# Conv-attention hybrid on one core: who takes the exponentials of the late rounds, where the gate's products stand, and the second norm in five chains

## The chip, the core and the metric

The kernel runs on one core of a Trainium2 chip: TensorE (matrix products, transposes), VectorE, ScalarE (functions from tables, copies), GpSimd and SyncE (transfers), each with its own queue in program order, joined by semaphores. The metric is the device time of one execution in microseconds. All data is float32.

## What is computed

Two images of 32 x 32 tokens with 128 channels go through three stages. The first is neighbourhood attention (7 x 7 window, 8 heads of 16 channels) with a gate and a layer norm; the second is additive attention, in which every pair of tokens of an image needs 32 tanh; the third sends each token to one of 8 experts.

```python
attn = jnp.einsum('bijnd,bijnpqd->bijnpq', q, kn) + bias
a = jax.nn.softmax(attn.reshape(B, H, W, NH, K * K), axis=-1)
out = jnp.einsum('bijnpq,bijnpqd->bijnd', a, vn).reshape(B, H, W, C) @ proj_w + proj_b
gate = jax.nn.sigmoid(jax.nn.relu(x @ g1_w + g1_b) @ g2_w + g2_b)
x = layernorm(x + out * gate) * ln_g + ln_b          # first norm
q, k = _ln_t(t) @ Wt, _ln_t(t) @ Wx                  # second norm
h = jnp.tanh(q[:, :, None, :] + k[:, None, :, :] + bh)
e = jnp.einsum('biju,u->bij', h, Wa[:, 0]) + ba[0]
t = t + softmax(e) @ _ln_t(t)
t = t + moe_ffn(_ln_t(t))                            # 8 experts, one per token
```

## The kernel before

**Rounds.** The neighbourhood attention goes by blocks of 128 queries, `NB` = 16, and each block in two rounds `rho` of four heads (`NG`), so 32 rounds (`NR`). A round takes scores of 128 queries with the 256 keys (blocks at an image's edge) or 320 keys around them. VectorE adds the bias table and finds the greatest of the sum in one instruction (`bias_score`, L1314: it writes minus the sum and, in `mn`, the least of that). ScalarE takes the exponential (`soften`, L1138), with `mn` as its bias. TensorE turns 128 x 128 pieces, two or three chunks of four heads (`turn_probs`), somebody copies them out of PSUM to `pts`, and TensorE multiplies by the values (`value_products`, L766). Then follow the sums of the heads, their inverse (VectorE), its spreading, the projection and the gated sum `y_all` (`gated`).

**First stage.** Rounds 0 to 15 (`RS` = 16, the first image) run alone. Ahead of them stand the projections (`project_in`, L682), the values and the gate's two small products (`gate_rows` L702, `gate_sums` L709), with a ReLU and a tanh by ScalarE after them.

**Steps.** Then comes a loop over steps `t`. Step `t` has unit `t` of the additive attention, of `T` = 128. A unit is 16 queries with the 1024 keys of their image: four tiles of 1024 columns, with 4 queries x 32 hidden channels on the partitions. GpSimd and VectorE form the sums of keys and queries three units ahead (`key_query_sums`, L604 and L1497) in a ring of `DEPTH` = 4 buffers. ScalarE takes the tanh in place (`hidden_units`, L1211: 4096 columns; in units 36 to 63, `HEAVY`, it forms a quarter itself with L1199). TensorE multiplies by the weights (`energies`, L924), which frees the ring's buffer (`h_used`). Eight units are a query block: its least (L1521), its exponential (L1229), its turn (`turn_main`, L950), the product with the tokens (`attend`, L961), the norm, the router and a scatter, each in a step of its own (`phase_step`, `query_block`).

**Late rounds.** Rounds 16 to 31 (the second image) are cut into steps between the units. `begin(rho)` is the step of the first pair of scores, the second pair is one step later (`score_pair`, `bias_pair`). ScalarE softens the pairs in steps `begin + 2` and `begin + 3`, after its tanh. The turns stand in steps `begin + 4` on (`turn_step`, one chunk a step), TensorE turns into bank 4 (`turn_probs_late`), VectorE copies it out (`turned_late`, L1341, `turn_copied`), and the values follow (`values_step`). Within a step TensorE has scores, values, sums, spreading, projection and the block's small products first, then the turn, then the energies of the step's unit. Small results go to bank 7 in turn, guarded by `misc_free`, which waits for VectorE's reads (`misc_read`) and for the row statistics that use bank 7 as scratch (`scratch_read`).

**Second norm.** Units from 64 on need the second image's tokens normed twice. `row_stats` and `scale_late` (VectorE: some dozen small instructions, each waiting for the one before) give mean and inverse root; `scale_rows`, `weigh_rows` and `normal_rows` (GpSimd) apply them. It goes in two groups of four blocks, from steps `middle` = 31 and `late_rows` = 53 on; keys of the last half are there in step 62, where the sums of units 64 and 65 are formed.

## Time and profile before

| | us |
|---|---|
| three runs | 681.07, 685.5, 685.56 (median 685.5) |
| profiled execution | 681.63 |
| its span | 679.8 |
| busy: TensorE, VectorE, ScalarE, GpSimd | 539.8, 489.3, 578.6, 478.5 |

The profile comes from one execution, the one of 681.63 us. Its page gives busy time by engine and by group of instructions; the views of the trace give single instructions in order of time, what ended each engine's idle time, and busy time by stretch. The granted TensorE clock is 1.00 at 2.4 GHz and 0.50 at 1.2 GHz. ScalarE is busy in 85% of the span and nearly always from 94 to 600 us.

### The profile page before, as it was taken

What the parts mean: (1) busy time and instruction counts of PE and PEld (TensorE: products, weight loads), DVE (VectorE), ACT (ScalarE), POOL (GpSimd) and SP (SyncE); (2) the same over time, 40 slices, a digit from 0 to 9 for tenths busy, and PEclk for the clock granted to TensorE, in tenths of its full rate; (3) what the DMA queues carried; (4) which work ended last, traced back from release to release, by engine and by line L of the source; (5) the groups of instructions that cost most, each with busy time, mean ns of one, the idle gap of its engine ahead of it and who ended that gap; (6) DMA issues with size and microseconds to landing.
All of it is one profiled execution on the core that took longest, in us unless ns stands there. A gap on an engine that the chain in (4) does not pass through costs nothing.

```text
span 679.8 us, 12439 instructions
## 1 busy us (share of the span) xinstructions
PE 539.8 (79%) x4560; PEld 268.5 (39%) x4560; DVE 489.3 (72%) x1395; ACT 578.6 (85%) x416; POOL 478.5 (70%) x545
## 2 busy tenths in 40 slices
PE   6898788989898979799868767676677668677993
PEld 3565444434443435354313223122222212337782
DVE  2677777878888887868756897878868787843456
ACT  3676569999999999999997999999999999970640
POOL 1002257997979779788997998879888887810565
PEclk9899899999999999899979799989989998998997
DMA  8600010100000000001700000000000000001400
GB/s 316 227 2 1 1 64 0 63 1 5 9 6 1 14 1 14 1 14 23 315 1 14 1 13 10 5 14 0 13 10 4 13 1 14 7 4 47 130 23 32
DMA packets 14108, 24.32 MB, mean 36 GB/s; under 512 B 1296, under 2 KB 11058, under 8 KB 13024
## 3 DMA queue, kind: packets, MB, share of 16 engines
q1 hardware_dynamic: 12640, 20.63, 8.8%
q0 software_dynamic: 1408, 2.91, 1.3%
q8 instruction: 36, 0.59, 0.4%
q14 instruction: 24, 0.20, 0.1%
HBM read 16.79 MB, written 7.37 MB: 36 GB/s over the span
## 4 chain that ended last, share of the span: by engine, by line
PE 33%; issue 22%; DVE 20%; ACT 18%; POOL 5%; DMA 1%; DVEq 0%; POOLq 0%; SPq 0%; ACTq 0%
ACT front L1211 16%; PE ps L924 9%; DVE front L1497 4%; POOL front L604 3%; PE ps L718 3%; PE ps L1092 3%; PE ps L1096 2%; DVE back L1314 2%; PE ps L961 2%; PE ps L747 2%; PE ps L766 2%; DVE back L1341 2%; PE ps L757 1%; PE ps L984 1%; PE ps L833 1%
## 5 line engine op out<-in xcount | busy, mean ns | idle before, releaser
L604 POOL TENSOR_SCALAR front<-k,q 128x1024 f32<-128x1024 f32 (+1 forms) x424 | 388.1, 934 | 50.2 <-PE ps L924 39.4
L1211 ACT ACTIVATE front<-front 128x4096 f32<-128x4096 f32 (+1 forms) x125 | 418.4, 3394 | 5.8 <-POOL front L604 5.8
L924 PE MATMUL ps<-front,cst 128*32 128x512 f32 x2032 | 254.2, 620 | 75.5 <-ACT front L1211 67.8
L1497 DVE TENSOR_SCALAR front<-ps,q 128x512 f32<-128x512 f32 x218 | 188.3, 902 | 22.7 <-PE ps L924 18.9
L924 PEld LDWEIGHTS ps<-front,cst 128*32 128x32 f32 x2032 | 54.8, 111 | 190.8 <-issue 95.8
L1138 ACT ACTIVATE back<-back,mn 128x320 f32<-128x320 f32 (+1 forms) x128 | 62.7, 540 | 15.2 <-DVE mn L1314 15.2
L1314 DVE CUSTOM_DVE_ANT_0 back<-ps,back 128x320 f32<-128x320 f32 (+1 forms) x128 | 54.0, 469 | 12.8 <-PE ps L718 11.5
L564 POOL TENSOR_SCALAR y_all<-y_all,mvs,lny 128x128 f32<-128x128 f32 x14 | 10.9, 788 | 72.1 <-DVEq L1470 59.5
L1529 DVE COPY ptm<-ps 128x512 f32<-128x512 f32 x31 | 21.4, 692 | 38.6 <-PE ps L950 37.4
L1199 ACT ACTIVATE front<-k,q 128x1024 f32<-128x1024 f32 (+1 forms) x50 | 45.8, 949 | 1.4 <-DVE k L1599 1.4
L718 PE MATMUL ps<-conv 32*128 32x320 f32 (+1 forms) x256 | 38.9, 487 | 4.2 <-DVE mn L1314 4.1
L1341 DVE COPY back<-ps 128x512 f32<-128x512 f32 x44 | 30.2, 687 | 10.3 <-PE ps L757 10.1
L619 POOL DMA_INDIRECT xbuf<-rec,slots x16 | 17.4, 1088 | 25.5 <-DVEq L1588 22.5
L961 PE MATMUL ps<-x_one,ptm 128*128 128x129 f32 x256 | 32.5, 279 | 1.3 <-DVE ptm L1529 1.3
L961 PEld LDWEIGHTS ps<-x_one,ptm 128*128 128x128 f32 x256 | 29.8, 191 | 9.4 <-issue 7.1
L747 PE MATMUL ps<-cst,back 128*128 128x128 f32 x176 | 27.7, 290 | 4.0 <-ACT back L1145 4.0
L660 POOL DMA_INDIRECT out<-front,dest x20 | 20.0, 999 | 14.3 <-DVE front L1753 9.6
L757 PE MATMUL ps<-cst,back 128*128 128x128 f32 x176 | 27.8, 280 | 1.2 <-DVE ptm L1529 1.2
L718 PEld LDWEIGHTS ps<-conv 32*128 32x128 f32 x256 | 15.0, 190 | 29.5 <-issue 16.7
L766 PE MATMUL ps<-back,conv 128*32 128x128 f32 x704 | 25.8, 276 | 1.1 <-DVE back L1333 0.6
L950 PEld LDWEIGHTS ps<-cst,pm 128*128 128x128 f32 x128 | 14.9, 152 | 29.1 <-issue 18.5
L1253 ACT ACTIVATE front<-ps 128x384 f32<-128x384 f32 (+1 forms) x8 | 3.0, 434 | 25.9 <-PE ps L1082 21.2
(152 smaller groups left out, 674.2 us busy)
## 6 DMA issues: line engine op xcount, KB each, us to landing
back<-in_w SPq DMA_DIRECT2D x2, 2048.0 KB, 10.9
xbuf<-rec SPq DMA_DIRECT2D x1, 2720.0 KB, 20.7
back<-in_top SPq DMA_DIRECT2D x2, 1024.0 KB, 5.7
back<-in_bottom SPq DMA_DIRECT2D x2, 1024.0 KB, 5.7
front<-xbuf SPq DMA_DIRECT2D x2, 720.0 KB, 7.4
back<-in_inner SPq DMA_DIRECT2D x1, 1280.0 KB, 9.8
back<-in_b SPq DMA_DIRECT2D x1, 1280.0 KB, 16.1
xT<-in_xT SPq DMA_DIRECT2D x4, 256.0 KB, 5.6
```

The lines of the kernel that those rows point to most:

```text
L604: last = nc.gpsimd.tensor_scalar(ring[u % DEPTH][:, at + lo:at + hi], k4[:, img * L + k0 + lo:img * L + k0 + hi], q4[:, m:m + 1], 1.0, ALU ...
L718: return nc.tensor.matmul(bank(to, 0, n), q_par[r][rows, at * P:(at + 1) * P], kT[rows, k0:k0 + n], start=True, stop=True)
L747: last = nc.tensor.transpose(bank(turn_bank(rho, c), g * P, (g + 1) * P), prob[rho % 3][:, g, c * P:(c + 1) * P], c_("ident"))
L766: last = nc.tensor.matmul(bank(6, r * P, (r + 1) * P)[g * HP:(g + 1) * HP, :], vals[:, value_block(j, c), 2 * g + r, :], pts[r][:, c, g * ...
L924: last = nc.tensor.matmul(bank(to)[c * U:(c + 1) * U, :], c_("wa", U - QPG - QPG * row, 2 * U - QPG - QPG * row), ring[t % DEPTH][:, at:at ...
L961: last = nc.tensor.matmul(bank(6, 2 * P, 2 * P + C + 1), ptm[:, k, :], x_one[:, p // BPI * BPI + k, :], start=(k == 0), stop=(k == BPI - 1))
L1138: nc.scalar.activation(p, p, ACT.Exp, bias=mn[rho % 3][:, g:g + 1], scale=-1.0).then_inc(p_ready, 1)
L1199: last = nc.scalar.activation(ring[t % DEPTH][:, at:at + keys], k4[:, k0:k0 + keys], ACT.Tanh, bias=q4[:, m:m + 1])
L1211: last = nc.scalar.activation(ring[t % DEPTH][:, 0:to], ring[t % DEPTH][:, 0:to], ACT.Tanh)
L1314: nc.vector.tensor_tensor_reduce(out=prob[rho % 3][:, g, 0:n], in0=bank(frm, 0, n), in1=btab[kind][:, 2 * g + r, :], scale=-1.0, scalar=3e ...
L1341: nc.vector.tensor_copy(pts[rho % 2][:, c, :], bank(4)).then_inc(turn_copied, 1)
L1497: last = nc.vector.tensor_scalar(ring[u % DEPTH][:, at + lo:at + keys], ps[:, base + k0 + lo:base + k0 + keys], q4[:, m:m + 1], None, ALU.add)
```

## The change

In the late rounds VectorE now makes two passes: the first as before (its written sum is not used any more), the second forms score plus bias less the greatest. TensorE turns that, and ScalarE takes the exponential from the turned columns in PSUM to `pts`; its softening of late rounds and VectorE's copies are gone. A last chunk of 64 keys is turned as 64 rows. Turns and all that follows of a round stand two steps earlier. In the first stage the gate's rows stand behind round 0's turns and its sums behind round 1's; `ones` is set first, and TensorE multiplies it ten times by itself before its first wait for data. The second norm of the second image goes in five chains (blocks 8 to 11, 12 and 13, 14, 15, with second statistics joined to the next group's first), most of GpSimd's parts one block a step, block 15 normed by VectorE at the end. Keys of the last half come in step 57.

```diff
-KEYS_1, TOKENS_2, KEYS_2 = 1, 46, 47
+KEYS_1, TOKENS_2, KEYS_2 = 1, 50, 51
...
-    gate = lambda u: KEYS_1 if u < NEW_KEYS[2] else project_step(NB - 1) + 9
+    gate = lambda u: KEYS_1 if u < NEW_KEYS[2] else project_step(NB - 1) + 6
...
-    return begin(rho) + 4 + c
+    return begin(rho) + 2 + c
...
-    return begin(rho) + 4 + CHUNKS[kind_of(rho // 2)]
+    return begin(rho) + 2 + CHUNKS[kind_of(rho // 2)]
...
-        middle, late_rows = project_step(11), project_step(NB - 1)
-        SCALES = (0, 0,
-                  middle + 2, middle + 8, late_rows + 1, late_rows + 4)
+        rows_8, rows_12, rows_14, rows_15 = (project_step(j) + 1 for j in (11, 13, 14, 15))
+        SCALES = (0, 0, rows_8 + 1, rows_12, rows_14, rows_15, rows_15 + 2)
...
+        def keys_in(rho, c):
+            return min(P, KEYS[kind_of(rho // 2)] - c * P)
...
-                if t == middle + 4:
-                    scale_rows(3, 8, 12)
-                if t == middle + 5:
+                if rows_8 + 2 <= t < rows_8 + 6:
+                    scale_rows(3, t - rows_8 + 6, t - rows_8 + 7)
+                if t == rows_8 + 6:
                     weigh_rows("lng", ALU.mult, 8, 12)
-                if t == middle + 6:
+                if t == rows_8 + 7:
                     weigh_rows("lnb", ALU.add, 8, 12, done=True)
-                if t == middle + 10:
-                    normal_rows(3, 8, 12)
-                if t == late_rows + 2:
-                    scale_rows(4, 12, NB)
-                    weigh_rows("lng", ALU.mult, 12, NB)
-                if t == late_rows + 3:
-                    weigh_rows("lnb", ALU.add, 12, NB, done=True)
-                if t == late_rows + 5:
-                    normal_rows(4, 12, NB)
+                if rows_12 < t <= rows_12 + 4:
+                    normal_rows(3, t - rows_12 + 7, t - rows_12 + 8)
+                if rows_12 < t <= rows_12 + 2:
+                    scale_rows(4, t - rows_12 + 11, t - rows_12 + 12)
+                if t == rows_12 + 3:
+                    weigh_rows("lng", ALU.mult, 12, 14)
+                if t == rows_12 + 4:
+                    weigh_rows("lnb", ALU.add, 12, 14, done=True)
+                if t == rows_14 + 1:
+                    scale_rows(5, 14, 15)
+                    weigh_rows("lng", ALU.mult, 14, 15)
+                    weigh_rows("lnb", ALU.add, 14, 15, done=True)
+                if rows_14 + 2 <= t < rows_14 + 4:
+                    normal_rows(4, t - rows_14 + 10, t - rows_14 + 11)
+                if t == rows_15 + 1:
+                    normal_rows(5, 14, 15)
+                    scale_rows(6, 15, NB)
+                    weigh_rows("lng", ALU.mult, 15, NB)
+                    weigh_rows("lnb", ALU.add, 15, NB, done=True)
...
+            pe.wait_ge(ones_ready, 1)
+            for _ in range(10):
+                nc.tensor.matmul(bank(7, 0, P), ones[:, :], ones[:, :], start=True, stop=True)
...
-                    pe.wait_ge(p_ready, NG * (rho + 1))
+                    pe.wait_ge(n_ready, NG * (rho + 1))
                 if probs_before(rho, c):
                     pe.wait_ge(turn_copied, probs_before(rho, c))
+                m = keys_in(rho, c)
                 for g in range(NG):
-                    last = nc.tensor.transpose(bank(4, g * P, (g + 1) * P), prob[rho % 3][:, g, c * P:(c + 1) * P],
+                    last = nc.tensor.transpose(bank(4, g * P, (g + 1) * P)[0:m, :], prob[rho % 3][:, g, c * P:c * P + m],
                                                c_("ident"))
                 last.then_inc(turn_done, 1)
...
-            pe.wait_ge(v_ready, 2)
-            gate_rows(7)
-            gate_sums(7)
             pe.wait_ge(k_ready, 2)
-            pe.wait_ge(v_ready, 3)
...
+                if rho == 0:
+                    pe.wait_ge(v_ready, 2)
+                    gate_rows(7)
+                if rho == 1:
+                    gate_sums(7)
...
+            def turned_late(rho, c):
+                act.wait_ge(turn_done, probs_before(rho, c) + 1)
+                if c == 0 and rho < RS + 2:
+                    act.wait_ge(pv_done, rho - 1)
+                elif c == 0:
+                    act.wait_ge(sixth_done, sixth_writes(values_step(rho - 2)) + 1)
+                m = keys_in(rho, c)
+                nc.scalar.activation(pts[rho % 2][0:m, c, :], bank(4)[0:m, :], ACT.Exp).then_inc(turn_copied, 1)
...
+                if turn_at(t):
+                    turned_late(*turn_at(t))
                 p = query_block(t, 2)
                 if p is not None:
                     soften_main(p)
-                rho = round_at(t - 2, begin)
-                if rho is not None:
-                    soften(rho, (0, 1))
-                rho = round_at(t - 3, begin)
-                if rho is not None:
-                    soften(rho, (2, 3))
...
+            nc.vector.memset(ones[:, :], 1.0).then_inc(ones_ready, 1)
...
             def bias_pair(rho, pair):
+
+                j, r = divmod(rho, 2)
+                kind, p = kind_of(j), prob[rho % 3]
+                n = KEYS[kind]
                 dve.wait_ge(pair_done, 2 * (rho - RS) + pair + 1)
-                for g in range(2 * pair, 2 * pair + 2):
-                    bias_score(rho, g, 2 + g % 2)
+                if pair == 0 and rho < RS + 3:
+                    dve.wait_ge(pt_done, chunks_before(rho - 2))
+                elif pair == 0:
+                    dve.wait_ge(turn_done, probs_before(rho - 3, CHUNKS[kind_of((rho - 3) // 2)] - 1) + 1)
+                heads = range(2 * pair, 2 * pair + 2)
+                for g in heads:
+                    last = nc.vector.tensor_tensor_reduce(out=p[:, g, 0:n], in0=bank(2 + g % 2, 0, n),
+                                                          in1=btab[kind][:, 2 * g + r, :], scale=-1.0, scalar=3e38,
+                                                          op0=ALU.add, op1=ALU.min, accum_out=mn[rho % 3][:, g:g + 1])
+                link(last)
+                for g in heads:
+                    nc.vector.scalar_tensor_tensor(p[:, g, 0:n], bank(2 + g % 2, 0, n), mn[rho % 3][:, g:g + 1],
+                                                   btab[kind][:, 2 * g + r, :], ALU.add, ALU.add).then_inc(n_ready, 1)
+                link.end()
...
-            def turned_late(rho, c):
-                dve.wait_ge(turn_done, probs_before(rho, c) + 1)
-                if rho < RS + 2:
-                    dve.wait_ge(pv_done, rho - 1)
-                else:
-                    dve.wait_ge(sixth_done, sixth_writes(values_step(rho - 2)) + 1)
-                nc.vector.tensor_copy(pts[rho % 2][:, c, :], bank(4)).then_inc(turn_copied, 1)
...
-                if t == middle + 1:
-                    dve.wait_ge(misc_read, misc_uses(middle + 1))
+                if t == rows_8:
+                    dve.wait_ge(misc_read, misc_uses(t))
                     row_stats(8, 12)
...
-                if t == middle + 7:
+                if t == rows_12:
+                    dve.wait_ge(misc_read, misc_uses(t))
                     dve.wait_ge(ln_rows, 3)
-                    row_stats(8, 12)
-                if t == middle + 8:
-                    scale_late(t, 8, 12)
+                    row_stats(8, 14)
+                    scale_late(t, 8, 14)
                     dve.sem_inc(ln_last, 1)
-                    link.end()
-                if t == late_rows - 1:
-                    row_stats(12, NB - 1)
-                if t == late_rows + 1:
-                    dve.wait_ge(misc_read, misc_uses(late_rows + 1))
-                    row_stats(NB - 1, NB)
-                    scale_late(t, 12, NB)
                     dve.sem_inc(ln_scale, 1)
                     link.end()
-                if t == late_rows + 4:
+                if t == rows_14:
+                    dve.wait_ge(misc_read, misc_uses(t))
                     dve.wait_ge(ln_rows, 4)
-                    row_stats(12, NB)
-                    scale_late(t, 12, NB)
+                    row_stats(12, 15)
+                    scale_late(t, 12, 15)
                     dve.sem_inc(ln_last, 1)
+                    dve.sem_inc(ln_scale, 1)
                     link.end()
+                if t == rows_15:
+                    dve.wait_ge(misc_read, misc_uses(t))
+                    dve.wait_ge(ln_rows, 5)
+                    row_stats(14, NB)
+                    scale_late(t, 14, NB)
+                    dve.sem_inc(ln_last, 1)
+                    dve.sem_inc(ln_scale, 1)
+                    link.end()
+                if t == rows_15 + 2:
+                    dve.wait_ge(ln_rows, 6)
+                    row_stats(15, NB)
+                    scale_late(t, 15, NB)
+                    link.end()
+                    normal_rows(x_all, 15, NB)
+                    dve.sem_inc(t_ready[3], 1)
```

ScalarE in the steps after the first query block: `L1211` (`L1232` of the changed kernel) is the tanh, `L1138` the exponential of two heads, `L1242` the new exponential of a chunk, with the semaphores that each waits for. Before:

```order
L1138 ACTIVATE back<-back,mn 128x320 [waits n_ready] x2
L1211 ACTIVATE front<-front 128x4096 [waits dve_sums,pool_sums]
L1138 ACTIVATE back<-back,mn 128x320 [waits n_ready] x2
L1211 ACTIVATE front<-front 128x4096 [waits dve_sums,pool_sums]
L1228 ACTIVATE pm<-pmh,nmin 128x512 [waits least_ready]
L1229 ACTIVATE pm<-pm,nmin 128x512
L1211 ACTIVATE front<-front 128x4096 [waits dve_sums,pool_sums]
L1138 ACTIVATE back<-back,mn 128x320 [waits n_ready] x2
L1211 ACTIVATE front<-front 128x4096 [waits dve_sums,pool_sums]
```

And in the changed kernel:

```order
L1232 ACTIVATE front<-front 128x4096 [waits dve_sums,pool_sums]
L1242 ACTIVATE back<-ps 128x512 [waits turn_done]
L1232 ACTIVATE front<-front 128x4096 [waits dve_sums,pool_sums]
L1242 ACTIVATE back<-ps 64x512 [waits turn_done]
L1258 ACTIVATE pm<-pmh,nmin 128x512 [waits least_ready]
L1259 ACTIVATE pm<-pm,nmin 128x512
L1232 ACTIVATE front<-front 128x4096 [waits dve_sums,pool_sums]
L1242 ACTIVATE back<-ps 128x512 [waits sixth_done,turn_done]
L1232 ACTIVATE front<-front 128x4096 [waits dve_sums,pool_sums]
L1242 ACTIVATE back<-ps 128x512 [waits turn_done]
```

Where two steps of three had a pair of exponentials that wait for VectorE's biases (`n_ready`), each step now has one that waits for TensorE's turn of the same step (`turn_done`).

VectorE in two steps with a pair of scores of an inner block: `L1497` (`L1528`) are key sums, `L1314` (`L1361`) the biases, `L1341` the copy of a turned chunk. Before:

```order
L1497 TENSOR_SCALAR front<-ps,q 128x512 [waits h_used]
L1497 TENSOR_SCALAR front<-ps,q 128x512
L1314 ISA back,mn<-ps,back 128x320 [waits pair_done]
L1314 ISA mn 128x1
L1314 ISA back,mn<-ps,back 128x320
L1314 ISA mn 128x1
L1341 COPY back<-ps 128x512 [waits pv_done,turn_done]
```

And in the changed kernel:

```order
L1528 TENSOR_SCALAR front<-ps,q 128x512 [waits v_ready,h_used]
L1528 TENSOR_SCALAR front<-ps,q 128x512
L1361 ISA back,mn<-ps,back 128x320 [waits pt_done,pair_done]
L1361 ISA mn 128x1
L1361 ISA back,mn<-ps,back 128x320
L1361 ISA mn 128x1
L1366 SCALAR_TENSOR_TENSOR back<-ps,mn,back 128x320 [waits dve_chain]
L1366 SCALAR_TENSOR_TENSOR back<-ps,mn,back 128x320
L123 ISA
```

The copy and its wait for the turn are gone; two passes over 320 columns stand behind the reductions.

TensorE in the first stage, from the last value rows (`L695`, `L711`) on: `L702` and `L709` (`L718` and `L725`) are the gate's products, `L718` (`L734`) scores, `L747` (`L763`) turns. Before:

```order
L695 MATMUL ps<-cst,xT 64x128
L702 MATMUL ps<-xT,cst 32x512 [waits ld_xT0,v_ready]
L702 MATMUL ps<-xT,cst 32x512 [waits ld_xT1]
L702 MATMUL ps<-xT,cst 32x512 [waits ld_xT2]
L702 MATMUL ps<-xT,cst 32x512 [waits ld_xT3]
L709 MATMUL ps<-cst,pm 128x4 [waits g1_ready]
L709 MATMUL ps<-cst,pm 128x4 x3
L718 MATMUL ps<-conv 128x256 [waits pads_ready,n_ready,v_ready,k_ready]
```

And in the changed kernel:

```order
L711 MATMUL ps<-cst,xT 64x128
L734 MATMUL ps<-conv 128x256 [waits n_ready,pads_ready,k_ready]
L734 MATMUL ps<-conv 128x256 x3
L763 MATMUL ps<-cst,back 128x128 [waits p_ready]
L763 MATMUL ps<-cst,back 128x128 x7
L718 MATMUL ps<-xT,cst 32x512 [waits ld_xT0,v_ready]
L718 MATMUL ps<-xT,cst 32x512 [waits ld_xT1]
L718 MATMUL ps<-xT,cst 32x512 [waits ld_xT2]
L718 MATMUL ps<-xT,cst 32x512 [waits ld_xT3]
L734 MATMUL ps<-conv 128x320 [waits n_ready]
```

The scores of round 1 now follow the value rows at once, and the gate's rows stand behind the turns of round 0.

## Rows read from the trace of the kernel before

**Rows 1.** Busy time by stretch: PE, PEld, DVE, ACT, POOL, then clock.

```profile
200.00:250.00 50.00, 41.83 (x395) 19.26 (x394) 43.04 (x132) 50.00 (x28) 43.84 (x49) 1.00 0.02 5
```

**Rows 2.** Timeline of ScalarE, steps 27 to 29: start, us, line [idle before].

```profile
216.74 1.01 ACT L1138 ACTIVATE back<-back,mn 128x320 f32<-128x320 f32 x2
217.63 7.13 ACT L1211 ACTIVATE front<-front 128x4096 f32<-128x4096 f32 x2
```

**Rows 3.** Timeline of TensorE, from energies 27 to the turn of step 28.

```profile
217.52 1.93 PE L924 MATMUL ps<-front,cst 128*32 128x512 f32 x16
219.67 0.66 PE L950 MATMUL ps<-cst,pm 128*128 128x128 f32 x4 [0.23 <-DVE back L1341]
220.25 0.81 PE L718 MATMUL ps<-conv 32*128 32x320 f32 x4
220.99 0.86 PE L766 MATMUL ps<-back,conv 128*32 128x128 f32 x24
221.79 0.66 PE L757 MATMUL ps<-cst,back 128*128 128x128 f32 x4
```

**Rows 4.** Timeline of ScalarE, units 62, 63 and 64.

```profile
360.41 2.75 ACT L1211 ACTIVATE front<-front 128x3072 f32<-128x3072 f32 x1
...
364.10 2.75 ACT L1211 ACTIVATE front<-front 128x3072 f32<-128x3072 f32 x1
371.64 10.63 ACT L1211 ACTIVATE front<-front 128x4096 f32<-128x4096 f32 x3 [4.79 <-POOL front L604]
```

**Rows 5.** Timeline of weight loads and products in the first stage.

```profile
8.91 0.34 PEld L682 LDWEIGHTS ps<-xT,cst 128*128 128x128 f32 x1 [0.52 <-issue]
...
10.08 0.19 PEld L682 LDWEIGHTS ps<-xT,cst 128*128 128x128 f32 x1 [0.24 <-issue]
...
16.67 1.07 PE L702 MATMUL ps<-xT,cst 128*32 128x512 f32 x8 [0.19 <-DVE conv L1301]
...
19.53 1.05 PE L718 MATMUL ps<-conv 32*128 32x256 f32 x8
20.51 1.97 PE L747 MATMUL ps<-cst,back 128*128 128x128 f32 x8
```

**Rows 6.** Groups by line and shape: busy us, mean ns, idle before.

```profile
L1138 ACT ACTIVATE back<-back,mn 128x320 f32<-128x320 f32 x96 | 48.4, 555 | 10.4 <-DVE mn L1314 10.4
L1314 DVE CUSTOM_DVE_ANT_0 back<-ps,back 128x320 f32<-128x320 f32 x96 | 42.1, 486 | 7.5 <-PE ps L718 6.3 <-DVE mvs L1398 0.5 <-DVE lny L139 0.3
...
L1341 DVE COPY back<-ps 128x512 f32<-128x512 f32 x44 | 30.2, 687 | 10.3 <-PE ps L757 10.1
...
L1145 ACT ACTIVATE back<-ps 128x512 f32<-128x512 f32 x28 | 16.5, 588 | 6.1 <-PE ps L747 5.9
...
L1138 ACT ACTIVATE back<-back,mn 128x256 f32<-128x256 f32 x32 | 14.3, 498 | 4.7 <-DVE mn L1314 4.7
...
L1314 DVE CUSTOM_DVE_ANT_0 back<-ps,back 128x256 f32<-128x256 f32 x32 | 11.9, 419 | 5.4 <-PE ps L718 5.2
...
L1378 DVE SCALAR_TENSOR_TENSOR y_all<-ps,gate,x_one 128x128 f32<-128x128 f32 x16 | 5.5, 346 | 1.1 <-PE ps L833 0.8 <-DVE lny L139 0.2
```

**Rows 7.** Timeline of VectorE, two of four biases of round 3.

```profile
27.28 0.49 DVE L1314 CUSTOM_DVE_ANT_0 back<-ps,back 128x320 f32<-128x320 f32 x1
...
27.69 0.49 DVE L1314 CUSTOM_DVE_ANT_0 back<-ps,back 128x320 f32<-128x320 f32 x1
```

**Rows 8.** Timeline of TensorE, steps 37 and 43.

```profile
263.75 0.71 PE L833 MATMUL ps<-cst,otn 128*128 128x128 f32 x4
264.30 1.95 PE L961 MATMUL ps<-x_one,ptm 128*128 128x129 f32 x16
...
283.31 0.61 PE L790 MATMUL ps<-cst,ots 128*128 128x4 f32 x4
```

**Rows 9.** Timeline of TensorE, step 34, behind the row statistics.

```profile
250.06 0.36 PE L978 MATMUL ps<-oh,cst 128*128 128x8 f32 x2 [2.68 <-DVEq L1414]
...
251.06 2.90 PE L924 MATMUL ps<-front,cst 128*32 128x512 f32 x16
```

More of the change, by code:

```diff
@@ L1165, in _ @@
             soften(0, range(NG))
-            act.wait_ge(g1_done, 1)
-            nc.scalar.activation(g1, bank(7), ACT.Relu, bias=c_("bg1")).then_inc(g1_ready, 1)
             for rho in range(RS):
@@ L1184, in _ @@
                     turned(rho, 2)
+                if rho == 0:
+                    act.wait_ge(g1_done, 1)
+                    nc.scalar.activation(g1, bank(7), ACT.Relu, bias=c_("bg1")).then_inc(g1_ready, 1)
+                if rho == 1:
+                    act.wait_ge(gz_done, 1)
+                    nc.scalar.activation(gt[:, :].rearrange("p (g k) -> p k g", g=NG),
+                                         bank(7, 0, NB).rearrange("p (k g) -> p k g", g=NG), ACT.Tanh,
+                                         bias=hg2b[:, :], scale=0.5).then_inc(gt_ready, 1)
             act.wait_ge(q4_done, 1)
@@ L1438, in _ @@
             value_rows(2, 6)
-            nc.vector.memset(ones[:, :], 1.0)
             for rho in range(RS):
```

30 lines of the change are left out of this document (12 added, 18 removed).

## The prediction

> **What bounds the kernel now.** Three stages matter: the first sixteen attention rounds (0 to about 94 us), units 0 to 63 of the key sums with the sixteen late rounds between them (about 94 to 367), and units 64 to 127 (372 to 600). I first read the busy time by stretch. From 200 to 250 us ScalarE is busy for all 50.00 us, VectorE for 43.04, GpSimd for 43.84 and TensorE for 41.83 [rows 1]. So in the middle stage ScalarE's work is the bound, and the others are 12 to 17% below it. Next the timeline of ScalarE: two tanh over 4096 columns take 7.13 us, so one is 3.61 long, the next starts 0.1 before its end and costs 3.51; a pair of exponentials of a late round takes 0.89 from its start to that of the tanh (216.74 to 217.63) [rows 2]. ScalarE never waits there for the rounds. The timeline of TensorE shows why that works although TensorE is late: its step is energies of the last unit, turned weights, a pair of scores, values, a turn, and then energies again [rows 3]. The turn of step 28 ends at 222.4 [rows 3], while tanh 28, which began at 217.63, ended at 221.2 [rows 2]. TensorE runs about 1 us behind ScalarE and nobody cares, because ScalarE asks only for sums made three units ahead. That slack is what the change touches. At the switch to the second image ScalarE stands still for 4.79 us [rows 4]: tanh 63 ends at 366.85, tanh 64 starts at 371.64, after keys that came late. The second half is all ScalarE and unchanged.
>
> **The start (terms: -1.5, -2.9, -0.9, +1.1).** The projections begin when xT lands. Their weight loads are 0.34 us and one every 0.86 at first, 0.19 and one every 0.43 from about 9.7 us on [rows 5]: TensorE's clock rose only then. Five to six of the twelve instructions run at half clock, so a full clock from the beginning is worth 5 x 0.43 = 2.1. The ten products of ones are 20 instructions over 128 columns; eight such at half clock take 1.97 us [rows 5], 0.25 each. From about 1 us on they make 4.9 us and end near 5.9, instead of the 5.3 at which the projections now begin: 0.6 back. Term -1.5.
> The gate's products now stand between value rows and the scores of round 1: from 16.67 (gate rows) to 19.53 (scores) [rows 5] is 2.86 us, half of it round trips to ScalarE. They leave: -2.9. The turns of round 0 ran at half clock after that pause, in 1.97 us [rows 5]; at full clock they are half of it: -0.9 if the pause is gone. The gate rows come back ahead of the scores of round 2, with 1.07 us [rows 5]: they would be hidden behind VectorE's biases only in part, and I charge +1.1. The gate sums in round 1 lie under VectorE's four biases of round 2; if that cover is gone they cost up to 0.5. Sum for the start: -4.2. All later work depends on it, so it is kept.
>
> **ScalarE's work in the late rounds (term -6.0).** Out: 64 exponentials, 48 over 320 columns and 16 over 256, 555 and 498 ns long [rows 6]. From start to start they are 0.1 less [rows 2], 0.45 and 0.40: 48 x 0.45 + 16 x 0.40 = 28.0. In: 44 exponentials from PSUM over 512 columns (12 of them on 64 partitions, which changes no duration). The nearest row is ScalarE's copy of the same shape, 588 ns long [rows 6], 0.49 with that overlap. I take 0.50, so 22.0. Net -6.0; with the full 0.59, where a wait stands ahead of it, it would be -2.0. The Trainium skill ("ScalarE: Activation LUTs", What ACT_TABLE_LOAD costs) says that every function costs the same per element and that an activation without a pointer operand takes 186 ns plus 0.833 per column; as an estimate from that page the new one is 0.61, less 0.09 of overlap 0.52, and the net would be -5.1.
>
> **VectorE (nothing by itself).** Out: 44 copies, 687 ns [rows 6], 0.60 from start to start, 26.4 in all, and with them the waits for a turn. In: 64 passes of score plus bias less greatest. Not in the trace; the same instruction over 128 columns is 346 ns, and the reduction grows from 256 to 320 columns by 67 ns, 1.05 ns a column (419 and 486) [rows 6], so 0.55 and 0.48 long. The reductions start 0.41 apart though 0.49 long [rows 7]. With that overlap the new ones are 0.47 and 0.41: 29.1 in all. Net +2.7 over 44 steps, below ScalarE's total. But a step with a pair now has 1.0 more and one copy less, and what follows on VectorE (inverse, row statistics) comes that much later. Bounds: 29.1, or without any overlap 34.1 plus about 0.1 for each of 32 semaphore waits, 37.
>
> **The new wait (terms +12.1, +3.0).** In every step 4 to 47 ScalarE does its tanh and then waits for that step's turn; behind it stand the next tanh and the exponentials of finished blocks. The turn stands behind everything TensorE has in the step, and TensorE starts the step with energies that need the tanh before. So each of the 44 steps now takes the longer of ScalarE's own time, 3.51 + 0.50 = 4.01 (from unit 36 on 3.69 + 0.50 = 4.19 [rows 4]), and TensorE's. The ring of four units no longer evens this out. TensorE's parts from start to start: energies 1.86, scores 0.74, values 0.80, turn 0.58, turned weights 0.58 [rows 3], projection 0.55, sums 0.46, the attended block 1.80 [rows 8]. Most steps give 3.2 to 3.9 and fit. Five do not, those with an attended block: steps 13 and 37 with 1.86 + 0.74 + 1.80 + 0.58 = 4.98 (0.97 and 0.79 over), 21 and 45 with the sums too, 5.44 (1.43 and 1.25), 29 with values and projection instead of scores, 5.59 (1.58). Together 6.0.
> Then VectorE's chains of row statistics. TensorE's next product in bank 7 waits for them; before, this cost TensorE 2.68 us at 250 [rows 9] and ScalarE nothing. Now the chain is in step 31, after steps 30 and 31 that have bias pairs with 1.0 more each: TensorE waits in step 32 and ScalarE with it, 2.7. The chain in step 42 covers six rows and stands ahead of the biases of step 43, on which the turn of 44 waits: 1.9, from 4.2 us of statistics and chain less a step's slack of about 2. That of step 48 comes after the last turn and costs nothing. Small misfits (value rows in steps 4 and 5, three steps at the edge) 1.5. Sum 6.0 + 2.7 + 1.9 + 1.5 = 12.1.
> After the wait at 250 the energies took 2.90 instead of 1.93 us [rows 3, 9], at half clock for some 4 us. Two such waits, 1.5 each with the turns beside them: +3.0. This is from none to 5.
>
> **The switch (term -4.8).** The last block's rows are final two steps earlier, the tail of the norm is one row instead of four, and keys come at step 57, not 62. The sums of unit 64 need them at 61, so four steps (15 us) cover what is left: the 4.79 goes. The five chains are the same arithmetic in smaller pieces; GpSimd has the room even where its load is highest, 43.84 of 50 us [rows 1].
>
> **Sum.** -4.2 - 6.0 + 12.1 + 3.0 - 4.8 = +0.1. The profiled execution took 681.6 us (span 679.8), so 681.7. The three runs were 681.07, 685.5 and 685.56; their median is 3.9 above the profiled one. I put the forecast at 685.
>
> **Rivals.** (a) The waits are smaller: TensorE keeps a full clock and VectorE, rid of its own waits for turns (10.3 us before the copies [rows 6]), is early enough for the chains. Then only 6.0 remains, and the sum is -4.2 - 6.0 + 6.0 - 4.8 = -9.0, 676.5 from the median. For it: GpSimd and VectorE have 12% to spare in the stage. Against: both chains stand in steps that are full. (b) Slower: VectorE becomes the bound. It decides from the point where a pair costs 2.1 instead of 1.8 us, when its mean step, which I add up to about 3.95, passes 4.01. With 37 instead of 29.1 us of new passes, 8 more lie on the path: 693. Against it is the overlap that the reductions show [rows 7]. The Trainium skill ("VectorE: DVE Perf Modes", The DRAIN you can't avoid) says that the pipeline empties after every operation and that one should keep their number small; by that the 64 added operations would cost more than their durations, and (b) would be the case. The page itself excepts operations that are not held, and the rows here show a next one 0.08 us before the end. (c) The gap at the switch stays, since another late piece takes its place: 690. (d) The start brings nothing, because the products of ones end too late or a transfer is waited for: 688 to 689.
>
> **Chances.** Forecast 0.45, (a) 0.27, (b) 0.15, (c) 0.06, (d) 0.07. About 1% (6.9 us) is what a measurement of this kernel can tell from no change. Below 678.6 lies most of (a): 0.25. Above 692.4 lies most of (b) and the far tail of the waits: 0.18. Between: 0.57. The range 674.5 to 694 takes in (a) with a cheaper clock and (b) at its price.
>
> **What would show it.** In the profile after: ScalarE's waits for turns in steps 4 to 47, near 12 to 15 us in sum and longest at the five attended blocks and the two chains; no wait of ScalarE for GpSimd near the switch; the scores of round 2 at about 18.2 instead of 22.4; ScalarE's new exponential near 0.6 us; VectorE's new pass near 0.55. I would be wrong if ScalarE waits in most steps (then VectorE or TensorE is the bound) or nearly never.

## The result, and the profile after

The changed kernel takes 698.2 us (median; 695.16 to 699.72) beside 683.6 us for the kernel before on the same chip. The ratio is 1.021, 95% interval 1.015 to 1.027. It is slower, by 14.6 us of the medians; the forecast was 685, no change beside the median of 685.5 that I had then. The profiled executions, 697.9 us (span 696.1) and 681.6 (span 679.8), differ by 16.3, and the account below is made between these two.

ScalarE's row says nearly all. These are lines of the changed kernel's page of grouped instructions (busy us, mean ns of one, idle time ahead of them and its releaser). Line 1232 is the tanh, 1242 ScalarE's new exponential, 1366 VectorE's new pass.

```profile
L1232 ACT ACTIVATE front<-front 128x4096 f32<-128x4096 f32 (+1 forms) x125 | 419.3, 3399 | 0.0
...
L1242 ACT ACTIVATE back<-ps 128x512 f32<-128x512 f32 (+1 forms) x44 | 25.9, 588 | 31.1 <-PE ps L774 30.7
...
L1366 DVE SCALAR_TENSOR_TENSOR back<-ps,mn,back 128x320 f32<-128x320 f32 (+1 forms) x64 | 31.3, 530 | 1.1
```

The durations came as forecast (588 ns and 530 ns; I had said 0.6 and 0.55 us). The 4.79 us of [rows 4] are gone: no idle time stands before a tanh any more. But ScalarE stands still for 30.7 us before its new exponential, where I had added up 15.1 (12.1 and 3.0 for the clock). The busy time of 200 to 250 us, which answers to [rows 1]:

```profile
200.00:250.00 50.00, 40.27 (x391) 19.03 (x384) 42.36 (x135) 45.11 (x23) 41.36 (x47) 1.00 0.02 6
```

Columns are the stretch, its length, and busy us of TensorE, its weight loads, VectorE, ScalarE and GpSimd, the granted clock (1.00), and the share and rate of DMA. ScalarE fell from 50.00 to 45.11, VectorE from 43.04 to 42.36. No engine is full now: the stage is bound by waits, not by a load.

**The account, between the two profiled executions.** I mark three points of ScalarE's timeline: the first key-sum tile, tanh 64, and the end.

| | before | after | difference | forecast |
|---|---|---|---|---|
| start, to the first key-sum tile | 94.61 | 89.51 | -5.1 | -4.2 |
| middle, ScalarE's work | 271.3 | 266.5 | -4.8 | -6.0 |
| middle, ScalarE standing still | 5.8 | 30.7 | +25.0 | +15.1 - 4.8 |
| rest, from tanh 64 on | 308.2 | 309.4 | +1.2 | 0 |
| span | 679.8 | 696.1 | +16.3 | +0.1 |

ScalarE's middle is 277.0 us before and 297.2 after, and its work in it is that less the time it stood still (5.77 and 30.7; all 5.77 before were for GpSimd's sums). The rest scatters: 307.4 to 309.4 us in the fourteen kernels that were profiled, so the +1.2 is not explained and need not be. The first tile scatters too: 92.3 to 95.7 us in kernels without the start part, 87.7 to 90.4 in those with all of it.

**Where the 30.7 us are** (idle time ahead of each exponential, read off ScalarE's timeline):

| place | after | forecast |
|---|---|---|
| entry: steps 4 and 5 | 7.29 + 3.91 = 11.2 | a part of "small misfits 1.5" |
| five attended blocks | 1.57 + 1.40 + 1.59 + 1.00 + 1.06 = 6.6 | 6.0 |
| chain in step 31 | 3.25 + 2.20 = 5.5 | 2.7, and 1.5 for the clock |
| chain in step 42 | 3.17 + 2.11 = 5.3 | 1.9, and 1.5 for the clock |
| others | 0.81, 0.75 and three under 0.35, 2.2 in all | a part of "small misfits 1.5" |

**The entry.** ScalarE's timeline after:

```profile
107.77 5.02 ACT L1220 ACTIVATE front<-k,q 128x512 f32<-128x512 f32 x8
120.09 0.60 ACT L1242 ACTIVATE back<-ps 128x512 f32<-128x512 f32 x1 [7.29 <-PE ps L774]
120.58 3.61 ACT L1232 ACTIVATE front<-front 128x4096 f32<-128x4096 f32 x1
128.10 0.60 ACT L1242 ACTIVATE back<-ps 128x512 f32<-128x512 f32 x1 [3.91 <-PE ps L774]
```

The eight tiles at 107.77 are unit 4, done at 112.7, and then comes step 4's exponential. TensorE in that time (energies 944, scores 734, value rows 711, turn 774):

```profile
106.88 0.70 PE L734 MATMUL ps<-conv 32*128 32x256 f32 x4
107.51 1.93 PE L944 MATMUL ps<-front,cst 128*32 128x512 f32 x16
110.84 0.70 PE L734 MATMUL ps<-conv 32*128 32x256 f32 x4 [1.40 <-DVE back L1366]
111.47 1.16 PE L711 MATMUL ps<-cst,xT 128*128 128x128 f32 x8
112.56 1.92 PE L944 MATMUL ps<-front,cst 128*32 128x512 f32 x16
114.41 0.70 PE L734 MATMUL ps<-conv 32*128 32x256 f32 x4
115.04 1.16 PE L711 MATMUL ps<-cst,xT 128*128 128x128 f32 x8
118.97 1.08 PE L774 MATMUL ps<-cst,back 128*128 128x128 f32 x4 [2.77 <-DVEq L1697]
119.98 3.64 PE L944 MATMUL ps<-front,cst 128*32 128x512 f32 x16
```

The scores of the first late round start at 106.88, and its first turn at 118.97: twelve us from a standing start. TensorE waits for VectorE twice in them. And VectorE, in the lines that answer (the first norm's last rows 1451, keys 1630, value rows 1328):

```profile
102.76 0.75 DVE L1451 TENSOR_SCALAR x_one<-y_all,mvs,lny 128x128 f32<-128x128 f32 x1
...
106.99 0.69 DVE L1630 COPY k<-ps 128x512 f32<-128x512 f32 x1 [0.68 <-PE ps L871]
...
109.91 0.88 DVE L1366 SCALAR_TENSOR_TENSOR back<-ps,mn,back 128x256 f32<-128x256 f32 x2
...
118.08 0.68 DVE L1328 TENSOR_TENSOR conv<-ps,cst 128x512 f32<-128x512 f32 x1
```

VectorE comes out of the first norm at 103.5 and has the keys at 107.7. From there on it is filled with hardly a pause: sums, two pairs of passes, value rows, a least of scores, sums, passes, value rows. The four passes of the first late round are done at 113.7 (the second pair starts at 112.82), so what holds its turn at the last is something else. The turn shares its bank with the value rows of the same step and can only come after VectorE's copy of them (118.76), which stands in VectorE's queue behind the passes of the next round. TensorE stands still for that copy for 2.77 us ahead of this turn, and for 1.43 ahead of step 5's. Before the change the same lateness was there. The first turn of a late round (line 757) was that of step 6, and came when ScalarE had just done tanh 6; nothing in ScalarE's queue asked for it. TensorE and then ScalarE, before:

```profile
126.67 0.66 PE L757 MATMUL ps<-cst,back 128*128 128x128 f32 x4
```

```profile
122.89 3.61 ACT L1211 ACTIVATE front<-front 128x4096 f32<-128x4096 f32 x1
126.40 0.90 ACT L1138 ACTIVATE back<-back,mn 128x256 f32<-128x256 f32 x2
```

Now the turn of step 4 is asked for at 112.7. ScalarE had run on to unit 4 ahead of TensorE, and the wait of 7.29 takes that lead away. After TensorE's 2.77 us of idle time the granted clock is 0.50 from 119 to 124 us: the energies took 3.64 instead of 1.92 and the scores 1.20 instead of 0.70. With the 1.43 for the value rows that is 3.65, most of the 3.91 of step 5.

**The chain in step 42.** TensorE, then VectorE, then ScalarE:

```profile
299.06 0.70 PE L734 MATMUL ps<-conv 32*128 32x256 f32 x4
303.85 1.06 PE L774 MATMUL ps<-cst,back 128*64 128x128 f32 x4 [4.09 <-DVE ptm L1560]
```

```profile
298.26 1.26 DVE L1428 BATCH_NORM_STATS2 bns<-y_all 128x6 f32<-128x128 f32 x6 [0.31 <-DVE osum L1620]
...
302.43 0.16 DVE L139 SCALAR_TENSOR_TENSOR lny<-ps,lny 128x6 f32<-128x6 f32 x1
303.10 0.69 DVE L1560 COPY ptm<-ps 128x512 f32<-128x512 f32 x1 [0.50 <-DVE lny L139]
```

```profile
304.95 0.59 ACT L1242 ACTIVATE back<-ps 64x512 f32<-64x512 f32 x1 [3.17 <-PE ps L774]
```

Statistics and roots take from 298.26 to 302.59, as long as forecast (4.2). The waiting instruction is another than I had named: step 43's turn, held by the copy of the finished block's turned weights out of the same bank, which stands behind the chain in VectorE's queue. The bank is free only when that copy is done. The granted clock is 0.50 from 303 to 307 us, and the energies behind the turn take 3.64. In step 32, behind the chain of step 31, TensorE waits as I had named it, for the row statistics themselves, but for 3.81 us and not 2.7:

```profile
249.59 0.30 PE L988 MATMUL ps<-cst,rec 128*128 128x128 f32 x1 [3.81 <-DVEq L1447]
```

### The profile page after: what moved, and what is told of

The parts are those of the page before. It is cut to its first block, busy times and chain, and to the rows that moved or that the text cites. A ratio compares the mean times of both kernels' runs of the same rounds, so it can differ in the third digit from the quotient of the medians.

```text
span 696.1 us, 12515 instructions
## 1 busy us (share of the span) xinstructions
PE 546.5 (78%) x4580; PEld 273.9 (39%) x4580; DVE 496.0 (71%) x1428; ACT 573.4 (82%) x396; POOL 477.4 (69%) x548
## 4 chain that ended last, share of the span: by engine, by line
PE 31%; ACT 28%; issue 22%; DVE 17%; POOL 0%; DVEq 0%; POOLq 0%; ACTq 0%
ACT front L1232 24%; PE ps L944 8%; DVE front L1528 3%; PE ps L734 2%; PE ps L1116 2%; PE ps L1112 2%; PE ps L763 2%; PE ps L783 2%; PE ps L981 2%; PE ps L1004 1%; ACT front L1220 1%; DVE back L1361 1%; PE ps L774 1%; ACT pm L1259 1%; PE ps L850 1%
## 5 line engine op out<-in xcount | busy, mean ns | idle before, releaser
L1232 ACT ACTIVATE front<-front 128x4096 f32<-128x4096 f32 (+1 forms) x125 | 419.3, 3399 | 0.0
L1528 DVE TENSOR_SCALAR front<-ps,q 128x512 f32<-128x512 f32 x218 | 188.3, 902 | 32.0 <-PE ps L944 29.1
L1242 ACT ACTIVATE back<-ps 128x512 f32<-128x512 f32 (+1 forms) x44 | 25.9, 588 | 31.1 <-PE ps L774 30.7
L1158 ACT ACTIVATE back<-back,mn 128x320 f32<-128x320 f32 (+1 forms) x64 | 31.3, 539 | 13.4 <-DVE mn L1339 13.4
L734 PE MATMUL ps<-conv 32*128 32x320 f32 (+1 forms) x256 | 39.3, 490 | 2.3 <-DVE back L1366 2.3
L774 PE MATMUL ps<-cst,back 128*128 128x128 f32 (+1 forms) x176 | 28.3, 284 | 8.9 <-DVE ptm L1560 4.6
L981 PEld LDWEIGHTS ps<-x_one,ptm 128*128 128x128 f32 x256 | 29.8, 191 | 10.8 <-issue 9.3
L1366 DVE SCALAR_TENSOR_TENSOR back<-ps,mn,back 128x320 f32<-128x320 f32 (+1 forms) x64 | 31.3, 530 | 1.1
L673 POOL DMA_INDIRECT out<-front,dest x20 | 19.8, 990 | 15.1 <-DVE front L1792 10.0
L763 PE MATMUL ps<-cst,back 128*128 128x128 f32 x176 | 27.5, 289 | 1.4 <-ACT back L1165 1.3
L1361 DVE CUSTOM_DVE_ANT_0 back<-ps,back 128x320 f32<-128x320 f32 (+1 forms) x64 | 27.5, 467 | 0.0
L734 PEld LDWEIGHTS ps<-conv 32*128 32x128 f32 x256 | 15.2, 192 | 29.4 <-issue 17.5
```

The lines of the kernel that those rows point to most:

```text
L734: return nc.tensor.matmul(bank(to, 0, n), q_par[r][rows, at * P:(at + 1) * P], kT[rows, k0:k0 + n], start=True, stop=True)
L763: last = nc.tensor.transpose(bank(turn_bank(rho, c), g * P, (g + 1) * P), prob[rho % 3][:, g, c * P:(c + 1) * P], c_("ident"))
L774: last = nc.tensor.transpose(bank(4, g * P, (g + 1) * P)[0:m, :], prob[rho % 3][:, g, c * P:c * P + m], c_("ident"))
L981: last = nc.tensor.matmul(bank(6, 2 * P, 2 * P + C + 1), ptm[:, k, :], x_one[:, p // BPI * BPI + k, :], start=(k == 0), stop=(k == BPI - 1))
L1158: nc.scalar.activation(p, p, ACT.Exp, bias=mn[rho % 3][:, g:g + 1], scale=-1.0).then_inc(p_ready, 1)
L1232: last = nc.scalar.activation(ring[t % DEPTH][:, 0:to], ring[t % DEPTH][:, 0:to], ACT.Tanh)
```

## The experiments

All are compared with the kernel before, run beside them on the same chip (its medians there were 682.2 to 684.0). "Waits" is what the trace shows of ScalarE's idle time ahead of the late exponentials. The rows from "lag of one tanh" on start from the changed kernel. "One chunk attended" and the last row have only two executions each.

| run | us, median | ratio to before, 95% | span of the profile | waits |
|---|---|---|---|---|
| start alone | 674.7 | 0.984 to 0.993 | 674.5 | none |
| norm alone | 679.3 | 0.993 to 0.999 | 681.0 | none |
| late rounds alone | 699.1 | 1.020 to 1.031 | 697.9 | 29.6 |
| ones alone | 677.9 | 0.990 to 0.996 | 676.1 | none |
| start and norm | 675.3 | 0.985 to 0.994 | 671.0 | none |
| changed kernel | 698.2 | 1.015 to 1.027 | 696.1 | 30.7 |
| lag of one tanh | 690.5 | 1.002 to 1.019 | 689.1 | 24.5 |
| one chunk attended | 694.0 | 1.008 to 1.024 | 693.8 | 27.4 |
| no chains | 687.3 | 1.004 to 1.011 | 682.5 | 19.9 |
| rounds two steps later | 686.8 | 1.001 to 1.008 | 684.9 | 18.6 |
| lag and two steps later | 680.1 | 0.994 to 0.998 | 675.3 | 13.5 |
| no second pass | 686.7 | 1.003 to 1.009 | 684.1 | 21.9 |
| two steps later, no chains, one chunk | 672.0 | 0.981 to 0.988 | 669.5 | 6.3 |

**Which part costs.** The first five take the change apart; their edits are pieces of the diff above. The start alone:

> The kernel before with the start part alone: ten products of ones, gate's products behind the turns. My forecast for this part was -4.2 us; the trace of the whole change has the first tanh of the key sums 5.1 us earlier. If parts add up, this kernel is 4 to 5 us faster than before, about 0.993. If the start brings something only together with the late part, it is within 1 us.

It gives more than forecast, 7.5 us of the medians. The first key-sum tile stands at 87.74. The products of ones alone:

> The kernel before with the ten products of ones alone, gate's products in their old place. My term was -1.5 us; the trace of the change has the last projections 2.2 us earlier. Expected: key sums begin 1.5 to 2.2 us earlier than in the kernel before (92.4 to 93.1 instead of 94.6), the rest unchanged, 680 us. The other part of the start would then be the gate's products, with 3 to 5 us.

677.9 us, and the first tile at 90.67. In the medians the ones alone are 5.1 us faster than the kernel before, and the whole start 7.5. Since the first tile scatters, the split is better read where each part has just acted. The scores of round 2 start at 22.41 us before, at 20.41 with the ones alone, at 17.08 with the whole start (16.88 in the changed kernel; I had expected 18.2). So the ones bring 2.0 up to there and the gate's products 3.3. TensorE with the ones alone (gate sums 713, scores of round 1 722, turns of round 0 751):

```profile
17.12 1.05 PE L713 MATMUL ps<-cst,pm 128*128 128x4 f32 x8 [0.81 <-ACT pm L1171]
18.10 0.71 PE L722 MATMUL ps<-conv 32*128 32x256 f32 x8
18.75 1.09 PE L751 MATMUL ps<-cst,back 128*128 128x128 f32 x8
```

The turns are at full clock (1.09, before 1.97 [rows 5]) although the gate's pause of 0.81 is still ahead of them. So the 0.9 for the turns belonged to the ones, not to the gate's products, and the scores (0.71, before 1.05) came with them. The norm alone:

> The kernel before with the second norm's five chains alone, the late rounds as they were. ScalarE's 4.79 us of standing still at the switch go and nothing else changes on ScalarE: -4.8 us, ratio 0.993. The rival says that the chains themselves make waits: then ScalarE waits elsewhere and the gain is under 2 us.

679.3 us, 2.9 below the kernel before. The gap at the switch went, but that did not bring its 4.8. The list of ScalarE's waits in the middle of this kernel (sum, times, longest) has others instead:

```profile
ACT front L1220 <- POOL front L603: 1.8, 5, 0.6
...
ACT front L1220 <- DVE front L1506: 1.6, 2, 1.3
```

That is 3.4 us; 1.0 of this kind stood in the kernel before too. ScalarE's middle is 276.1 instead of 277.0 (the profile is of an execution of 682.9 us; the ten lie from 677.4 to 683.9). The chain of step 50 (step 48 in the changed kernel) holds TensorE for 4.08 us here. The longest of these waits, 1.29, is a few us behind it, and I read it so that VectorE's sums wait for TensorE to free the ring, and ScalarE for the sums. The late rounds alone:

> The kernel before with the late rounds alone (subtraction on VectorE, exponentials of turned columns on ScalarE), start and norm as they were. The theory (ScalarE's wait for each step's turn stands in its queue ahead of the next tanh) gives -6 us of ScalarE's work and +22 to +31 us of waits, so +16 to +25 us, of which 10 to 12 in steps 4 and 5; a gap at the switch stays near 4.8. If the chains of the norm in their new places made most of the loss, this kernel is under +8.

699.1 us: the whole loss is in this part. Its middle is 297.3 us, that of the full change 297.2, and this kernel has no gap at the switch either, although it has the old norm. So the new norm isn't needed to close it. The late rounds alone have a part in their edit that can: values and projection of every round stand two steps earlier, and the old norm starts from the last projection, so its keys come in step 60 and not in 62. VectorE copies them at 381.98, 7.6 us ahead of tanh 64 (389.63); in the kernel before it did at 367.87, 1.0 after tanh 63 had ended. That is a shift of 8.6 us, and two steps are 7.4. Each part closes the gap without the other. Start and norm together:

> The kernel before with start and norm, and without the late part: what the change would be without its largest part. By sums of the two parts -9 to -10 us, ratio 0.986, faster than both kernels. ScalarE has no wait for turns, since it has none in its queue. If instead the late part is what hides the others' costs, this is nearer to 1.0.

675.3 us, 6.9 below the kernel before where I had expected 9 to 10; the start alone takes 674.7. With the start in place the norm's five chains bring nothing that the medians show. Both beat the kernel before and the changed one; the start alone is the simplest that does.

**What the 30.7 us are.** ScalarE's exponential one tanh later, the same work on every engine:

```
-                if turn_at(t):
-                    turned_late(*turn_at(t))
+                if turn_at(t - 1):
+                    turned_late(*turn_at(t - 1))
```

> The changed kernel with one edit: ScalarE does the exponential of a step's turn after the next step's tanh, one place later in its queue. Every engine has the same work. The theory (the 31 us are ScalarE's in-order wait for the turn, with no lead left) says that one step of lead covers the attended blocks and the chains and most of the entry: 31 us become under 9, the kernel takes 673 to 678 us, 20 to 25 under the changed one. The rival (VectorE's second pass and its load are the cost) says that nothing changes: 696 to 700 us, with the waits ahead of other instructions.

690.5 us: a third of what I expected of it. The rival as I had put it (nothing changes) is out, since moving one instruction in a queue took 6 us of waits. But my size was wrong. I read it so that the lag gives a lead only to a TensorE that isn't late already, and after the entry it is (4.04 + 3.92 + 1.18 there). There is also a price that I had not seen. All turns use one bank, so TensorE now waits for ScalarE in its list of waits:

```profile
PE ps L970 <- ACT back L1242: 3.5, 3, 1.9
```

The rounds two steps later:

```
-BEGIN = dict(zip(range(RS, NR), [2, 4] + [6 + 3 * k for k in range(12)] + [42, 44]))
+BEGIN = dict(zip(range(RS, NR), [4, 6] + [8 + 3 * k for k in range(12)] + [44, 46]))
-ENTRY = 8
+ENTRY = 10
```

> The changed kernel with all late rounds two steps later (and the value rows where they were). The theory says that the 11.2 us at the entry (steps 4 and 5) come from VectorE still being in the first norm's last rows at 94 to 107 us, so that two steps (7 to 8 us) take away 7 to 11 of them, while attended blocks and chains still cost 8 to 13: 687 to 691 us. If the entry wait belongs to the first round's own length (scores, two passes, turn in 12 us from a standing start), it moves with the rounds and the time stays at 698.

686.8 us. The entry's 11.2 us are 1.2 now. So they came from where the first late turns stood in the program. The edit does two things there: the turns are asked for two steps later (the first comes at 121.34 instead of 118.97), and they no longer share steps 4 and 5 with the value rows, which stayed. It doesn't part the two; the trace of the changed kernel puts 2.77 of the 7.29 and 1.43 of the 3.91 on TensorE's wait for the value rows' copy. Both edits together:

> The changed kernel with both edits that gave something: the late rounds two steps later, and ScalarE's exponential one tanh later. With the lag alone, TensorE was already a step behind after the entry and never caught up (waits 24.5 us). If the lead of a step holds once the entry is out of the way, the attended blocks (6 us) go and the chains are halved: waits from 18.6 with the shift alone to 8 or less, 676 us. If the one bank for turns ties TensorE to ScalarE anyway (its next turn waits for that exponential), the lag adds 2 us at most: 684 to 686.

680.1 us, 18 under the changed kernel and 3 under the one before. The lead holds in part (13.5 us of waits). This is also the nearest that the late part came to paying: the start alone is 5 us faster without it. Among TensorE's waits, those for VectorE's second pass have grown from 2.3 (3 times) in the changed kernel to 5.9:

```profile
PE ps L734 <- DVE back L1366: 5.9, 8, 2.2
```

The chains replaced by two memsets each (part of the computation left out), and the attended product at one chunk:

```
-                    row_stats(12, 15)
-                    scale_late(t, 12, 15)
+                    stats_left_out(12, 15)
+                    scale_left_out(t, 12, 15)
```

> The changed kernel, but VectorE's row statistics and inverse roots of the second norm are replaced by two memsets for each chain (part of the computation left out). The theory says that the waits of 5.45 us at steps 31 and 32 and of 5.28 us at steps 42 to 44 go, half clock after them included, and that the entry and the attended blocks stay: 9 to 11 us less, 687 to 689. If the half clock comes from something else, only 5 to 6 go.

```
-                for k in range(BPI):
+                for k in range(BPI if t > 50 else 1):
```

> The changed kernel, but the attended product of steps 13 to 45 has one of its eight chunks (part of the computation left out; each is 1.6 us shorter on TensorE). The theory says that the waits of 1.57, 1.40, 1.59, 1.00 and 1.06 us at these five steps go and all other waits stay: 6.6 us less, 691 us. The rival (ScalarE is held by VectorE) leaves them as they are.

Without the chains 687.3 us and 19.9 us of waits: 10.8 less. Of the chains' 10.7 us, with the half clock behind them, 1.1 are left (0.62 and 0.44), so 9.7 went there; the entry had 1.0 less in this execution. At one chunk 694.0 us: the waits at the attended blocks went, but only 3.3 of the 6.6 us are a net gain. The entry had 2.0 more in this execution, 0.4 to 0.7 more came at each of four other places, and 0.8 less at one. A half of it moved on, then; whether into other waits or by the scatter of the entry, one execution can't tell. VectorE's second pass left out, with ScalarE's exponential at a scale of -1:

```
-                link(last)
-                for g in heads:
-                    nc.vector.scalar_tensor_tensor(p[:, g, 0:n], bank(2 + g % 2, 0, n), mn[rho % 3][:, g:g + 1],
-                                                   btab[kind][:, 2 * g + r, :], ALU.add, ALU.add).then_inc(n_ready, 1)
-                link.end()
+                    last.then_inc(n_ready, 1)
```

> The changed kernel without VectorE's second pass (part of the computation left out: the 64 passes of score and bias less greatest; ScalarE's exponentials are of unsubtracted sums), all else in its place. VectorE has some 29 us less to do. The rival (VectorE's second pass is the cost) says that most of the 31 us of waits go: 675 us or less. The theory says that the passes lie beside other work but for the entry (8 passes of 0.4 ahead of the first turns) and the chains behind full steps: 4 to 9 us less, and the attended blocks' 6.6 us stay: 688 to 692 us.

686.7 us, a little under my interval, and 21.9 us of waits:

```profile
L1242 ACT ACTIVATE back<-ps 128x512 f32<-128x512 f32 (+1 forms) x44 | 25.8, 587 | 22.0 <-PE ps L774 21.9
```

31 us of VectorE's work taken away bring 8.8 of waits: 3.3 at the entry (5.23 and 2.72 are left), 5.4 at the chains (1.32, 0.53, 2.26 and 1.17 are left), 0.7 at the attended blocks, and one other wait is 1.1 longer. So VectorE's load is a part of the price where it stands on the way to a turn, and is not the bound. The rounds two steps later, without the chains, at one chunk:

> The changed kernel with the late rounds two steps later, the norm's chains replaced by memsets and the attended product at one chunk of eight (the last two leave out part of the computation). The three causes together should account for the 31 us of waits: under 5 us left, 668 to 672 us. If another wait takes the place of each, 10 or more are left.

6.3 us of waits are left of 30.7, and 672.0 us. The three causes account for 24 of the 31. I had expected under 5 left; the remaining waits are 1.41 and less, and I didn't look into them. ScalarE's work in this middle is 272.3 - 6.3 = 266.0, against 271.3 before: this 5.3 is what the late part could bring at most.

## Why the prediction was wrong, by its own steps

**What bounds the kernel**: right. ScalarE did bound the middle, with TensorE behind it, and "that slack is what the change touches" was the point.

**The start, -4.2**: -5.1 in the profiled pair, and 7.5 of the medians alone. At the scores of round 2 it was 5.3 to 5.5. The terms were near: up to the value rows the ones brought 1.4 alone and 2.0 with the whole start (term -1.5), and the gate's products and turns came as added up. The scores at full clock (0.3) and a wait of some 0.2 for VectorE ahead of the gate's rows, which went, came on top. That the turns' 0.9 hung on the gate's pause was wrong: it came with the ones alone. One reading is less sure than I wrote it: over the first projections of the kernel before, the granted clock reads 1.00, so the half clock there shows in the durations only.

**ScalarE's work, -6.0**: -4.8 to -5.3. An exponential behind a wait loses the overlap of 0.1 with the tanh before it, and there were sixteen.

**VectorE, nothing by itself**: durations right (547 ns for 320 columns), rival (b)'s mechanism wrong: VectorE is busy for 42.36 of 50 us, and two passes of 480 ns take 0.88 from the first's start to the second's end, so nothing is added between them. (The Trainium skill, "VectorE: DVE Perf Modes", The DRAIN you can't avoid, says that the pipeline is flushed after every operation, and excepts a next one that is not held; these rows are as the exception has it.) But "nothing" is not right either. Without the passes 8.8 us of waits go. The kernel went to the slow side, as (b) has it, but 5 us beyond (b)'s 693 and by another way.

**The new wait, +12.1 and +3.0**: the step that failed; the waits were 30.7 us. Its parts fared differently. The attended blocks, worked out as the longer of two sums in each step, were right (6.6 for 6.0). The two chains were at the right places, but 10.7 instead of 7.6 with the clock; for the second I named the biases as the way to the turn, and it was the shared bank. The term that broke the forecast is "small misfits (value rows in steps 4 and 5 ...) 1.5". It was 11.2 at steps 4 and 5 alone, 9.7 us more than the whole term. I compared loads step by step as if both engines began each step together. I never asked where VectorE stands when the first late round begins, and the trace before would have shown it: the first turn of a late round there came at 126.67, when ScalarE was in step 6. The change asks for that turn in step 4 and lets ScalarE wait for it. I did name the value rows of steps 4 and 5, but as a load; that the turn waits for VectorE's copy of them out of the shared bank (2.77 and 1.43 us of TensorE) was in no term.

**The switch, -4.8**: the gap went, so the term stands in the sum rightly. I gave three reasons for it, rows two steps earlier, a shorter tail and earlier keys; the first is enough in the late rounds alone, and so are the other two in the norm alone. And where the norm alone was changed it did not pay 4.8 but 2.9 in the medians and 1.0 in the profile (277.0 to 276.1), with 3.4 us of waits for sums at other places, where I had the chains as free. Rival (c) did not come.

**The sum, put right**: +0.1; the entry 9.7 more than the whole term of misfits; the chains 3.1; the attended blocks 0.6; the other small waits 2.2; less 1.0 for small waits of before that I hadn't counted. That is 14.7. With ScalarE's work 1.2, the start -0.9 and the rest 1.2 it makes 16.2 of the 16.3 in the profiles. The upper end of my range, 694, was (b) at its price; no case in it had the lead lost at the entry.

## What to carry to other kernels

When an instruction that waits is put into the queue of the engine that sets the pace, its wait is no longer paid out of the buffers between the engines: compare not only the load of each step, but where the producer stands in time at the first step. Read the time of the first such product in the trace before, and start the waiting part only after it, or one place later in the queue. A wait may also come from a bank shared with other work of the same step: look for what else is written there. And a gap that each of two parts of a change closes can be counted only once.

## What the runs showed of the hardware

The ten products of ones did more than start the clock early. In the kernel before, scores and turns at 19.53 and 20.51 us took 1.05 and 1.97 us [rows 5], after the pause of 0.81 at the gate's sums; the granted clock is 0.77 from 19.5 to 20 us and 0.50 from there to 23. With the ones ahead of the projections the same pause was there, they took 0.71 and 1.09, and the granted clock is 1.00 in every stretch up to 23 us. TensorE kept its full clock over the same gap when it had been busy from 1 us on. What it is in the earlier work that decides this, these runs don't tell. Later, after TensorE had stood still for 2.77 us, 16 energies took 3.64 us instead of 1.92, at a granted clock of 0.50.

The exponential took 585 ns on 64 partitions and 589 on 128, over the same 512 columns. VectorE's new pass took 547 ns for 320 columns and 480 for 256, and a second pass behind the first started 0.08 us before the first ended.
